# Handing x over already turned, and starting the matmul operands at differing byte offsets, in a conditional FFN kernel

## The chip, the cores and the metric

The kernel runs on one core of one Trainium2 chip. The metric is device time in microseconds (us), the median of several runs; lower is better. The engines are PE (matmul, with PEld its weight loads), DVE (vector), ACT (scalar and activation), POOL (GpSimd) and SP, which in this kernel only issues DMAs. The code is written engine by engine: each engine has its own program, and the programs meet only through semaphores, so the order inside an engine is the order written.

## The reference, cut to what matters

```
B, T, D = 4, 1024, 1024;  8 groups of LATENT = 128 columns;  FFN = 512
h    = gelu(einsum('btel,elf->btef', x as 8 groups, W1) + b1)
y    = einsum('btef,efl->btel', h, W2) + b2                  # back to D = 1024
eo   = silu(cond) @ emb_W + emb_b;   scale, shift = halves of eo
hn   = layernorm(y, ln_g, ln_b) * (1 + scale) + shift
out  = x + silu(hn) @ out_W + out_b
```

Everything is float32. To keep precision the kernel splits each matmul operand into a rounded high part (float32r) and a low rest, and does three matmuls in place of one: high by high, low weights by high, high weights by low.

## The kernel before

**Two parts.** The first part (FFN) makes y, turned so that the 128 columns of a group lie on the partitions and the tokens run along the row. It goes over 4 blocks of 1,024 tokens, one for each batch entry; in each block over 8 groups g; in each group over 4 chunks c of the 512 hidden columns. k = 4g + c counts the 32 steps of a block. Each step has on PE a `first` (W1, 6 matmuls of 512 columns into a PSUM ring slot) and a `second` (W2, 6 matmuls of 512 columns into the y PSUM), with `first` two steps ahead of `second`. The blocks are FIRST, two rounds of MIDDLE in a hardware loop, and LAST. Between the two matmul sets ACT does the gelu (L510) and DVE splits its result into g_hi (L664) and g_lo (L666); at the end of a group ACT adds b2 and writes y_stage (L543), and SP stores it to DRAM (L364).

The second part (projection) goes over 8 windows of 512 tokens with 4 row tiles each. A tile is 48 matmuls of 512 columns (L964; L977 for the last tile). There the weights loaded into the array are slices of s_hi and s_lo (128 tokens), and the moving operands are oW_hi and oW_lo. Mean and variance of the next window are two pairs of matmuls with ones_r as weights (L852, L853).

**How x gets turned.** x lies in DRAM with a token to a row. `load_x` (L303) brings a group of a block as 8 pieces of 128 tokens by 128 columns into `xin`. At k = 0 of each group PE turns the next group: `turn_x` (L820), 8 matmuls against an identity into a ring slot of its own. ACT copies that slot to `xT_raw` (L502), then rounds it to `xT_hi` (L506); DVE makes `xT_lo` (L659). There are 31 such turns: 8 start in FIRST, 16 in MIDDLE, 7 in LAST. The very first group is turned in two halves ahead of everything (L869, copied at L519, rounded at L521, rest at L650), and its matmuls are at L883. The small vectors (b1, b2, emb_b, ln_g, ln_b, cond) come in as 104 rows by six DMAs, are turned once on PE (L873) and copied to `cols` (L654).

**Other work with an order of its own.** In FIRST, SP loads the raw weights of a group two groups ahead, ACT rounds them (L533) and POOL makes the low part (L425). POOL does this in one loop: for group m it first waits for y_stage of group m - 2 and adds it to a running sum (L443), and only then splits the weights of group m. PE waits for that split before the first matmul of group m (at k = 2 of the group before). In LAST, POOL, ACT and DVE also normalise window 0 while PE still works on the FFN: SP loads y of window 0 back in two halves (L356), issued at k = 4 and k = 8 behind the load of x, and POOL centres it (L469), adds up squares (L474) and scales it (L481).

**The SP queue at the start of a group.** At k % 4 == 0 SP waits for a count of `xT_psum`, which PE raises when a turn is complete, then issues the next load of x. In LAST the load of y (L356) stands behind that wait.

**Where operands lie.** SBUF tensors are placed one after the other in the order of the `sb` calls, each at a multiple of 32 bytes. From the sizes in the code, the start of each tensor taken modulo 512 bytes is: oW_hi, oW_lo and ident 128; ones_r 32; sum_hi, sum_lo 64; and W, xT_hi, xT_lo, g_hi, g_lo, xin, and in the second part s_hi and s_lo of both windows, all 448. Every slice that a matmul takes begins a multiple of 512 bytes after the start of its tensor.

Of the kernel before, what the change touches and what calls it, by code (L numbers as in the profile page):

```python
# [5 lines left out]
P = 128  # L25
F32 = mybir.dt.float32
# [8 lines left out]
def cond_ffn_program(nc, x, cond, W1, b1, W2, b2, emb_W, emb_b, ln_g, ln_b, out_W, out_b, out):  # L35
# [3 lines left out]
    KE = cond.shape[1] // P  # L39
    NE = emb_W.shape[1] // P  # L40
    TA = T
    SUB = TA // P
# [18 lines left out]
    assert ROWS <= P  # L61

    with ExitStack() as ctx:
# [9 lines left out]
        oW_hi = sb("oW_hi", [P, G, D], F32R)  # L73
        oW_lo = sb("oW_lo", [P, G, D], F32R)
# [12 lines left out]
        vec_rows = emb_rows[:, 0:P]  # L87
# [6 lines left out]
        with ExitStack() as a:  # L94

            W = sb("W", [P, G, 4, FF], F32R, a)
            xT_hi = sb("xT_hi", [P, 2, TA], F32R, a)
            xT_lo = sb("xT_lo", [P, 2, TA], F32R, a)
            g_raw = sb("g_raw", [P, 2, TA], F32, a)
            g_hi = sb("g_hi", [P, 2, TA], F32R, a)  # L100
            g_lo = sb("g_lo", [P, 2, TA], F32R, a)
            xT_raw = sb("xT_raw", [P, TA], F32, a)
            xin = sb("xin", [P, 2, SUB, P], F32, a)
            y_stage = sb("y_stage", [P, 2, TA], F32, a)
            wraw = sb("wraw", [P, 2, 2 * FF], F32, a)
            assert D == 2 * FF == KE * P


        with ExitStack() as b:
            yb0 = sb("yb0", [P, G, TB], F32, b)  # L110
            s_lo0 = sb("s_lo0", [P, G, TB], F32R, b)
            s_hi0 = sb("s_hi0", [P, G, TB], F32R, b)
            sq = sb("sq", [P, G, TB], F32, b)
            yb1 = sb("yb1", [P, G, TB], F32, b)
            s_hi1 = sb("s_hi1", [P, G, TB], F32R, b)
            s_lo1 = sb("s_lo1", [P, G, TB], F32R, b)
            res = sb("res", [P, 2, D], F32, b)
            out_b_all = sb("out_b_all", [P, D], F32, b)
# [14 lines left out]
        vec_landed_pool = sem("vec_landed_pool")  # L133
        vec_turned = sem("vec_turned")
        cols_ready = sem("cols_ready")
# [21 lines left out]
        x0T_psum = sem("x0T_psum")  # L157
        x0_raw = sem("x0_raw")
        x0_hi = sem("x0_hi")
        x0_lo = sem("x0_lo")  # L160
        xT_psum = sem("xT_psum")
        xraw_done = sem("xraw_done")
# [102 lines left out]
        x_cols = x.rearrange("b (s p) (g l) -> b g p s l", p=P, l=L)  # L265
# [13 lines left out]
        def landed(m):  # L279
# [7 lines left out]
        small_vectors = ((R_B1, b1.rearrange("g (c p) -> (g c) p", p=P)), (R_B2, b2),  # L287
                         (R_C, cond.rearrange("b (k p) -> (b k) p", p=P)),
                         (R_EB, emb_b.rearrange("(n p) -> n p", p=P)),
                         (R_G, ln_g.rearrange("(n p) -> n p", p=P)),  # L290
                         (R_B, ln_b.rearrange("(n p) -> n p", p=P)))

# [3 lines left out]
        def _(sp):  # L296
# [5 lines left out]
            def load_x(i, g):  # L302
                sp.dma_start(xin[:, g % 2], x_cols[i, g]).then_inc(x_landed[g % 2], 16)  # L303

            for h in range(2):
                part = slice(h * SB, (h + 1) * SB)
                sp.dma_start(xin[:, 0, part], x_cols[0, 0, :, part]).then_inc(x0_landed[h], 16)
            for r0, v in small_vectors[:3]:
                sp.dma_start(vec_rows[r0:r0 + v.shape[0], :], v).then_inc(vec_landed, 16)
# [104 lines left out]
        def _(pool):  # L414
# [5 lines left out]
            for r0, v in small_vectors[3:]:  # L420
                pool.dma_start(vec_rows[r0:r0 + v.shape[0], :], v).then_inc(vec_landed_pool, 16)
# [70 lines left out]
        def _(act):  # L492
# [20 lines left out]
            for h in range(2):  # L513
                part = slice(h * BANK, (h + 1) * BANK)
                if h == 0:
                    act.wait_ge(x0T_psum, 1)
                else:
                    act.wait_ge(xT_psum, 1)
                nc.scalar.copy(xT_raw[:, part], ring(0)[:, part]).then_inc(xraw_done if h else x0_raw, 1)  # L519
                act.wait_ge(xraw_done if h else x0_raw, 1)  # L520
                nc.scalar.copy(xT_hi[:, 0, part], xT_raw[:, part]).then_inc(xhi_done if h else x0_hi, 1)  # L521
            act.wait_ge(cols_ready, 1)
# [25 lines left out]
            def body(i, kind):  # L548
                start, last = kind == FIRST, kind == LAST
                slot, _ = PLAN[kind]  # L550
                for k in range(K):
                    g = k // C
                    if ("T", g + 1) in slot and k % C == 0:
# [76 lines left out]
        def _(dve):  # L630
# [16 lines left out]
            for h in range(2):  # L647
                part = slice(h * BANK, (h + 1) * BANK)
                dve.wait_ge(xhi_done if h else x0_hi, 1)
                nc.vector.tensor_tensor(xT_lo[:, 0, part], xT_raw[:, part], xT_hi[:, 0, part].bitcast(F32),  # L650
                                        ALU.subtract).then_inc(xlo_done if h else x0_lo, 1)
                if h == 0:
                    dve.wait_ge(vec_turned, 1)
                    nc.vector.tensor_copy(cols[:], psum[:, 4, 0:ROWS]).then_inc(cols_ready, 1)  # L654
            split_w0(1)

            def rest_xT(n, g):
                dve.wait_ge(xhi_done, n + 1)
                nc.vector.tensor_tensor(xT_lo[:, g % 2], xT_raw[:], xT_hi[:, g % 2].bitcast(F32),  # L659
# [30 lines left out]
            def body(i, kind):  # L690
                last = kind == LAST
                slot, _ = PLAN[kind]
                for k in range(K):
# [15 lines left out]
                    if ("T", g + 1) in slot and k % C == 0:  # L709
                        rest_xT(G * i + g + 1, (g + 1) % G)  # L710
# [106 lines left out]
        def _(pe):  # L817
            def turn_x(slot, g):
                for s in range(SUB):
                    mm = nc.tensor.transpose(ring(slot)[:, s * P:(s + 1) * P], xin[:, g % 2, s], ident[:])  # L820
                mm.then_inc(xT_psum, 1)

# [42 lines left out]
            pe.wait_ge(ident_ready, 1)  # L865
            for h in range(2):
                pe.wait_ge(x0_landed[h], 16)
                for s in range(h * SB, (h + 1) * SB):
                    mm = nc.tensor.transpose(ring(0)[:, s * P:(s + 1) * P], xin[:, 0, s], ident[:])  # L869
                mm.then_inc(xT_psum if h else x0T_psum, 1)  # L870
            pe.wait_ge(vec_landed, 16 * 3)
            pe.wait_ge(vec_landed_pool, 16 * 3)
            nc.tensor.transpose(psum[:, 4, 0:ROWS], vec_rows[0:ROWS, :], ident[0:ROWS, 0:ROWS]  # L873
                                ).then_inc(vec_turned, 1)
# [13 lines left out]
            def body(i, kind):  # L888
# [3 lines left out]
                def take(use):  # L892
# [4 lines left out]
                    elif kind == "T":  # L897
                        pe.wait_ge(xraw_done, G * i + n + 1)
# [8 lines left out]
                for k in range(K):  # L907
                    g = k // C
                    if k % C == 0 and ("T", g + 1) in slot:

                        if g + 1 < G:

                            pe.wait_ge(x_landed[(g + 1) % 2], 16 * ((G // 2) * i + g // 2 + 1))
                        else:
                            pe.wait_ge(x_landed[0], 16 * ((G // 2) * i + G // 2))
                        turn_x(take(("T", g + 1)), (g + 1) % G)
# [6 lines left out]
                    if last and k == K_TURN:  # L923
                        ps = ring(take(("F", 0)))
                        pe.wait_ge(emb_copied, KE + 1)
# [91 lines left out]
_INS = ["x", "cond_2048", "L0_cond_W1", "L0_cond_b1", "L0_cond_W2", "L0_cond_b2", "L0_cond_emb_W",  # L1017
        "L0_cond_emb_b", "L0_cond_ln_g", "L0_cond_ln_b", "L0_cond_out_W", "L0_cond_out_b"]


# [16 lines left out]
```

## Time and profile before

| | |
|---|---|
| device time, median of 3 runs | 799.18 us (798.22 to 799.32) |
| span of the profiled execution, first to last instruction | 788.0 us |
| what lies around the span, median less span | 11.2 us |
| PE busy | 764.1 us, 97% |
| DVE, ACT, POOL busy | 624.4, 365.5, 207.8 us |

The page gives no device time of the profiled execution itself, so the 11.2 us around its span are taken from the median. A row of a timeline begins with its start and its length in us, counted from the span's start. Matmuls overlap in the records (one of 512 columns is shown some 390 ns long), so the pace of a run of matmuls is read from start to start, or from the chain of work, which counts each piece once.

### The profile page before, as it was taken

The page shows a single profiled execution, that of the slowest core. Times are in us where ns is not written, and L with a number is a line of the kernel's source. Part 1 is how long each engine was busy: PE and PEld are TensorE (multiplying, and loading weights), DVE is VectorE, ACT ScalarE, POOL GpSimd, SP SyncE. Part 2 cuts the span into 40 slices and gives each one's busy share as a digit, 9 for nine tenths or more (in the row PEclk, how much of TensorE's full clock was granted, in tenths as well). Part 3 has the DMA queues.
Part 4 walks back from the last instruction along what each step waited for, and adds up shares of the span by engine and source line. Part 5 has one row for each costly group of instructions (what it writes and reads, how often), then busy time and mean ns, then how long its engine had stood idle before and what let it go on. Part 6 is the DMA issues. An engine that isn't in the chain of part 4 may idle for free.

```text
span 788.0 us, 9365 instructions
## 1 busy us (share of the span) xinstructions
PE 764.1 (97%) x3429; PEld 610.6 (77%) x3429; DVE 624.4 (79%) x492; ACT 365.5 (46%) x360; POOL 207.8 (26%) x110
## 2 busy tenths in 40 slices
PE   7999999999999999989988999999999999999998
PEld 5878788787787877866766887888888888888886
DVE  6888879778797786899898798888788788878511
ACT  6767567576675756566742323223041322314100
POOL 3344333022040220185162132122221221222111
PEclk9999999999999999999999999999999999999999
DMA  6353344445345453341227325252523425132221
GB/s 162 94 148 116 97 138 127 164 145 175 121 130 175 135 184 106 107 160 54 82 81 266 106 86 208 81 192 76 213 107 132 161 80 210 56 108 107 106 89 72
DMA packets 60720, 101.68 MB, mean 129 GB/s; under 512 B 2856, under 2 KB 39824, under 8 KB 58512
## 3 DMA queue, kind: packets, MB, share of 16 engines
q1 hardware_dynamic: 59920, 100.71, 37.4%
q10 hardware_dynamic: 672, 0.52, 0.2%
q8 instruction: 20, 0.33, 0.2%
q14 instruction: 12, 0.10, 0.0%
q0 software_dynamic: 96, 0.02, 0.0%
HBM read 67.69 MB, written 33.55 MB: 128 GB/s over the span
## 4 chain that ended last, share of the span: by engine, by line
PE 71%; issue 11%; DVE 9%; POOL 4%; ACT 2%; DMA 2%; SPq 0%; DVEq 0%; POOLq 0%; ACTq 0%
PE psum L964 39%; PE psum L831 13%; PE psum L845 13%; DVE g_hi L664 3%; POOL W L425 2%; PE psum L820 2%; PE psum L977 1%; DVE g_lo L666 1%; POOL stat L443 1%; PE psum L860 1%; DMA yb<-y_scratch 1%; DMA xin<-in_x 1%; DVE xT_lo L659 1%; DVE yb L765 1%; DVE sq L743 1%
## 5 line engine op out<-in xcount | busy, mean ns | idle before, releaser
L510 ACT ACTIVATE g_raw<-psum,cols 128x1024 f32<-128x1024 f32 x128 | 142.8, 1117 | 121.7 <-PE psum L831 91.4
L666 DVE TENSOR_TENSOR g_lo<-g_raw,g_hi 128x1024 fp32r<-128x1024 f32 x128 | 177.8, 1389 | 4.4
L488 POOL TENSOR_TENSOR res<-res,out_b_all 128x1024 f32<-128x1024 f32 x32 | 84.2, 2633 | 281.9 <-DMA res<-in_x 281.9
L964 PE MATMUL psum<-oW_hi,s_hi 128*128 128x512 f32 x496 | 156.2, 396 | 0.0
L964 PE MATMUL psum<-oW_lo,s_hi 128*128 128x512 f32 x496 | 156.1, 395 | 0.0
L964 PE MATMUL psum<-oW_hi,s_lo 128*128 128x512 f32 x496 | 156.0, 395 | 0.0
L831 PE MATMUL psum<-xT_hi,W 128*128 128x512 f32 x508 | 141.1, 400 | 4.9 <-POOL W L425 2.5
L845 PE MATMUL psum<-g_hi,W 128*128 128x512 f32 x512 | 137.2, 390 | 0.2 <-DVE g_hi L664 0.2
L664 DVE CAST g_hi<-g_raw 128x1024 fp32r<-128x1024 f32 x128 | 112.1, 876 | 30.7 <-PE psum L845 26.5
L831 PEld LDWEIGHTS psum<-xT_hi,W 128*128 128x128 f32 x508 | 92.1, 189 | 31.9 <-issue 6.9
L845 PEld LDWEIGHTS psum<-g_hi,W 128*128 128x128 f32 x512 | 96.0, 188 | 20.9 <-DVE g_hi L664 0.7
L964 PEld LDWEIGHTS psum<-oW_hi,s_hi 128*128 128x128 f32 x496 | 93.3, 188 | 22.9
L964 PEld LDWEIGHTS psum<-oW_lo,s_hi 128*128 128x128 f32 x496 | 93.2, 188 | 22.9
L964 PEld LDWEIGHTS psum<-oW_hi,s_lo 128*128 128x128 f32 x496 | 93.2, 188 | 22.9
L614 ACT ACTIVATE sq<-yb 128x2048 f32<-128x2048 f32 x14 | 26.9, 1920 | 132.7 <-DVE yb L760 132.7
L845 PE MATMUL psum<-g_lo,W 128*128 128x512 f32 x256 | 80.2, 394 | 5.7 <-DVE g_lo L666 5.7
L831 PE MATMUL psum<-xT_lo,W 128*128 128x512 f32 x254 | 78.3, 390 | 0.0
L755 DVE TENSOR_TENSOR res<-psum,res 128x1024 f32<-128x1024 f32 x31 | 37.9, 1221 | 46.7 <-PE psum L964 46.7
L659 DVE TENSOR_TENSOR xT_lo<-xT_raw,xT_hi 128x1024 fp32r<-128x1024 f32 x31 | 44.6, 1438 | 30.7 <-ACT xT_hi L506 30.7
L599 ACT ACTIVATE yb<-yb,mod_c,mod_a 128x512 f32<-128x512 f32 x64 | 47.0, 805 | 42.2 <-DVE yb L765 42.1
L425 POOL TENSOR_TENSOR oW_lo<-wraw,oW_hi 128x512 f32 x16 | 29.8, 1884 | 133.4 <-ACT oW_hi L588 133.4
L845 PEld LDWEIGHTS psum<-g_lo,W 128*128 128x128 f32 x256 | 47.2, 188 | 19.4 <-DVE g_lo L666 10.2
(97 smaller groups left out, 689.7 us busy)
## 6 DMA issues: line engine op xcount, KB each, us to landing
y_scratch<-y_stage SPq DMA_DIRECT2D x32, 512.0 KB, 3.3
res<-in_x SPq DMA_DIRECT2D x32, 512.0 KB, 3.3
xin<-in_x SPq DMA_DIRECT2D x31, 512.0 KB, 4.9
out<-res SPq DMA_DIRECT2D x31, 512.0 KB, 2.6
yb<-y_scratch SPq DMA_DIRECT2D x7, 2048.0 KB, 8.1
wraw<-in_L_cond_emb_W SPq DMA_DIRECT2D x8, 1024.0 KB, 5.0
wraw<-in_L_cond_out_W SPq DMA_DIRECT2D x8, 512.0 KB, 4.9
wraw<-in_L_cond_W SPq DMA_DIRECT2D x14, 256.0 KB, 3.7
```

The lines of the kernel that those rows point to most:

```text
L425: nc.gpsimd.tensor_tensor(lo, raw, hi.bitcast(F32), ALU.subtract).then_inc(pw_split, 1)
L488: nc.gpsimd.tensor_tensor(res[:, t % 2], res[:, t % 2], out_b_all[:], ALU.add).then_inc(res_biased, 1)
L510: nc.scalar.activation(g_raw[:, k % 2], ring(slot), ACT.Gelu, bias=cols[:, R_B1 + k:R_B1 + k + 1]).then_inc(gelu_done, 1)
L599: return nc.scalar.activation(yb[s][:, g], yb[s][:, g], ACT.Silu, scale=mod_a[:, b, g:g + 1], bias=mod_c[:, b, g:g + 1])
L614: nc.scalar.activation(sq[:, half], yb[s][:, half], ACT.Square).then_inc(squared, 1)
L659: nc.vector.tensor_tensor(xT_lo[:, g % 2], xT_raw[:], xT_hi[:, g % 2].bitcast(F32), ALU.subtract).then_inc(xlo_done, 1)
L664: nc.vector.tensor_copy(g_hi[:, s], g_raw[:, s]).then_inc(ghi_done, 1)
L666: nc.vector.tensor_tensor(g_lo[:, s], g_raw[:, s], g_hi[:, s].bitcast(F32), ALU.subtract).then_inc(glo_done, 1)
L755: nc.vector.tensor_tensor(res[:, t % 2], proj[t % 2], res[:, t % 2], ALU.add).then_inc(out_ready, 1)
L831: mm = nc.tensor.matmul(ring(slot)[:, h * BANK:(h + 1) * BANK], W[:, g, w, cut], v[:, g % 2, h * BANK:(h + 1) * BANK], start=(n == 0), sto ...
L845: mm = nc.tensor.matmul(y_psum(g % 2)[:, h * BANK:(h + 1) * BANK], W[:, g, w, cut], v[:, k % 2, h * BANK:(h + 1) * BANK], start=(c == 0 an ...
L964: mm = nc.tensor.matmul(proj[t % 2][:, h * BANK:(h + 1) * BANK], v[:, g, cut], w[:, g, h * BANK:(h + 1) * BANK], start=(g == 0 and n == 0) ...
```

## The change

x is handed to the kernel a second time, turned (`xT`, batch by group by column by token), and the small vectors as one array of 128 partitions by 104 (`vectors`); both are made before the launch. PE turns nothing of x or of the vectors any more. `xT_raw` becomes a double buffer which the DMA fills, in place of `xin`; ACT rounds from it as soon as the load has landed. SP's wait at the start of a group is for `xlo_done` (DVE has made xT_lo) in place of `xT_psum`. The ring in PSUM has no slot for turns. Besides, unused pieces (`gap0` to `gap7`) are put between tensors, and g_raw is moved behind g_lo.

```diff
@@ def cond_ffn_program
         oW_hi = sb("oW_hi", [P, G, D], F32R)
+        sb("gap0", [P, 16])
         oW_lo = sb("oW_lo", [P, G, D], F32R)
...
             W = sb("W", [P, G, 4, FF], F32R, a)
+            sb("gap1", [P, 16], F32, a)
             xT_hi = sb("xT_hi", [P, 2, TA], F32R, a)
+            sb("gap2", [P, 16], F32, a)
             xT_lo = sb("xT_lo", [P, 2, TA], F32R, a)
+            sb("gap3", [P, 32], F32, a)
+            g_hi = sb("g_hi", [P, 2, TA], F32R, a)
+            sb("gap4", [P, 72], F32, a)
+            g_lo = sb("g_lo", [P, 2, TA], F32R, a)
             g_raw = sb("g_raw", [P, 2, TA], F32, a)
-            g_hi = sb("g_hi", [P, 2, TA], F32R, a)
-            g_lo = sb("g_lo", [P, 2, TA], F32R, a)
-            xT_raw = sb("xT_raw", [P, TA], F32, a)
-            xin = sb("xin", [P, 2, SUB, P], F32, a)
+            xT_raw = sb("xT_raw", [P, 2, TA], F32, a)
...
             s_lo0 = sb("s_lo0", [P, G, TB], F32R, b)
+            sb("gap5", [P, 32], F32, b)
             s_hi0 = sb("s_hi0", [P, G, TB], F32R, b)
             sq = sb("sq", [P, G, TB], F32, b)
             yb1 = sb("yb1", [P, G, TB], F32, b)
+            sb("gap6", [P, 64], F32, b)
             s_hi1 = sb("s_hi1", [P, G, TB], F32R, b)
+            sb("gap7", [P, 96], F32, b)
             s_lo1 = sb("s_lo1", [P, G, TB], F32R, b)
@@ ring_plan
-                if k % C == 0 and not (last and k // C + 1 == G):
-                    uses.append(("T", k // C + 1))
@@ sync
             def load_x(i, g):
-                sp.dma_start(xin[:, g % 2], x_cols[i, g]).then_inc(x_landed[g % 2], 16)
+                sp.dma_start(xT_raw[:, g % 2], xT[i, g]).then_inc(x_landed[g % 2], 16)
...
-            for r0, v in small_vectors[:3]:
-                sp.dma_start(vec_rows[r0:r0 + v.shape[0], :], v).then_inc(vec_landed, 16)
+            sp.dma_start(cols[:], vectors).then_inc(vec_landed, 16)
...
-                        wait(xT_psum, G * i + g + 1)
+                        wait(xlo_done, G * i + g + 1)
@@ gpsimd
-            for r0, v in small_vectors[3:]:
-                pool.dma_start(vec_rows[r0:r0 + v.shape[0], :], v).then_inc(vec_landed_pool, 16)
@@ scalar
-            def copy_xT(n, slot):
-                act.wait_ge(xT_psum, n + 1)
-                nc.scalar.copy(xT_raw[:], ring(slot)).then_inc(xraw_done, 1)
-
-            def round_xT(n, g):
-                act.wait_ge(xraw_done, n + 1)
-                nc.scalar.copy(xT_hi[:, g % 2], xT_raw[:]).then_inc(xhi_done, 1)
+            def round_xT(i, g):
+                s = g % 2
+                act.wait_ge(x_landed[s], 16 * ((G // 2) * i + (g + s) // 2))
+                nc.scalar.copy(xT_hi[:, s], xT_raw[:, s]).then_inc(xhi_done, 1)
...
-                        act.wait_ge(xlo_done, G * i + g + 1)
-                        copy_xT(G * i + g + 1, slot["T", g + 1])
-                        round_xT(G * i + g + 1, (g + 1) % G)
+                        round_xT(i, g + 1)
@@ tensor
-            def turn_x(slot, g):
-                for s in range(SUB):
-                    mm = nc.tensor.transpose(ring(slot)[:, s * P:(s + 1) * P], xin[:, g % 2, s], ident[:])
-                mm.then_inc(xT_psum, 1)
...
-                        turn_x(take(("T", g + 1)), (g + 1) % G)
```

By the same count as above, after the change the starts modulo 512 are: oW_hi 128, oW_lo 192; W 0, xT_hi 64, xT_lo 128, g_hi 256, g_lo 32; s_lo0 0, s_hi0 128, s_hi1 384, s_lo1 256.

## Rows read from the trace of the kernel before

**Rows 1.** The page: engines, granted clock in slices, and the chain's shares.

```profile
PE 764.1 (97%) x3429; PEld 610.6 (77%) x3429; DVE 624.4 (79%) x492; ACT 365.5 (46%) x360; POOL 207.8 (26%) x110
...
PEclk9999999999999999999999999999999999999999
...
PE 71%; issue 11%; DVE 9%; POOL 4%; ACT 2%; DMA 2%; SPq 0%; DVEq 0%; POOLq 0%; ACTq 0%
```

**Rows 2.** The chain in order of time (start, us, what): MIDDLE, then the projection.

```profile
212.40 1.36 PE psum L845 x6
...
719.03 54.60 PE psum L964 x234
```

**Rows 3.** Timeline of PE in one group of MIDDLE, turn to turn.

```profile
209.53 0.62 PE L845 MATMUL psum<-g_lo,W 128*128 128x512 f32 x2
209.99 1.03 PE L820 MATMUL psum<-ident,xin 128*128 128x128 f32 x8
210.78 1.17 PE L831 MATMUL psum<-xT_hi,W 128*128 128x512 f32 x4
...
221.76 1.03 PE L820 MATMUL psum<-ident,xin 128*128 128x128 f32 x8
```

**Rows 4.** The chain in order of time, one round of FIRST.

```profile
80.91 7.08 issue
...
88.02 1.91 POOL stat L443
...
91.14 2.29 POOL W L425
```

**Rows 5.** Waits of PE for POOL (us, times, longest).

```profile
PE psum L831 <- POOL W L425: 2.5, 5, 0.7
```

**Rows 6.** Timeline of all engines, the opening.

```profile
4.81 1.09 PE L869 MATMUL psum<-ident,xin 128*128 128x128 f32 x4 [4.81 <-DMA xin<-in_x]
5.94 0.59 ACT L519 COPY xT_raw<-psum 128x512 f32<-128x512 f32 x1 [2.94 <-PE psum L869]
6.55 0.62 ACT L521 CAST xT_hi<-xT_raw 128x512 fp32r<-128x512 f32 x1
...
6.64 1.12 PE L869 MATMUL psum<-ident,xin 128*128 128x128 f32 x4 [0.74 <-DMA xin<-in_x]
...
7.88 1.19 PE L883 MATMUL psum<-xT_hi,W 128*128 128x512 f32 x2
...
9.21 1.28 ACT L526 ACT_TABLE_LOAD   x1
9.29 1.05 PE L883 MATMUL psum<-xT_hi,W 128*128 128x512 f32 x2
...
10.14 0.63 PE L883 MATMUL psum<-xT_lo,W 128*128 128x512 f32 x1
...
10.81 1.12 ACT L510 ACTIVATE g_raw<-psum,cols 128x1024 f32<-128x1024 f32 x1 [0.32 <-PE psum L883]
...
12.19 1.03 PE L820 MATMUL psum<-ident,xin 128*128 128x128 f32 x8
...
15.06 1.09 PE L845 MATMUL psum<-g_hi,W 128*128 128x512 f32 x4
```

**Rows 7.** Loads of x by tile, issue to landing.

```profile
DMA to landing us min/median/max: 3.9/4.9/6.7
```

**Rows 8.** Timeline of LAST around the load of y.

```profile
322.04 1.12 ACT L543 ACTIVATE y_stage<-psum,cols 128x1024 f32<-128x1024 f32 x1 [0.19 <-PE psum L845]
...
324.38 1.05 ACT L506 CAST xT_hi<-xT_raw 128x1024 fp32r<-128x1024 f32 x1
324.40 0.85 SPq L356 DMA_DIRECT2D yb<-y_scratch  x1
...
325.46 1.23 DVE L659 TENSOR_TENSOR xT_lo<-xT_raw,xT_hi 128x1024 fp32r<-128x1024 f32 x1 [1.46 <-ACT xT_hi L506]
```

**Rows 9.** Timeline of DVE in LAST, with POOL at work, and between.

```profile
353.09 2.19 DVE L666 TENSOR_TENSOR g_lo<-g_raw,g_hi 128x1024 fp32r<-128x1024 f32 x1
...
356.34 0.68 DVE L664 CAST g_hi<-g_raw 128x1024 fp32r<-128x1024 f32 x1
357.05 1.23 DVE L666 TENSOR_TENSOR g_lo<-g_raw,g_hi 128x1024 fp32r<-128x1024 f32 x1
358.19 1.78 DVE L664 CAST g_hi<-g_raw 128x1024 fp32r<-128x1024 f32 x1
```

**Rows 10.** Groups of instructions by line, ACT's copies (busy us, mean ns, idle before).

```profile
L502 ACT COPY xT_raw<-psum 128x1024 f32<-128x1024 f32 x31 | 31.5, 1017 | 6.1 <-ACT y_stage L543 6.1
```

More of the change, by code:

```diff
@@ L32, with cond_ffn_program @@
 LN_EPS = 1e-5
-def cond_ffn_program(nc, x, cond, W1, b1, W2, b2, emb_W, emb_b, ln_g, ln_b, out_W, out_b, out):
+def cond_ffn_program(nc, x, xT, vectors, W1, W2, emb_W, out_W, out_b, out):
     B, T, D = x.shape
@@ L38, in cond_ffn_program @@
     C = FF // P
-    KE = cond.shape[1] // P
+    KE = emb_W.shape[0] // P
     NE = emb_W.shape[1] // P
     TA = T
-    SUB = TA // P
     NA = B * T // TA
@@ L60, in cond_ffn_program @@
     ROWS = R_C + B * KE
-    assert ROWS <= P
+    assert vectors.shape[1] == ROWS
     with ExitStack() as ctx:
@@ L302, in load_x @@
             def load_x(i, g):
[L303 removed]
+                sp.dma_start(xT_raw[:, g % 2], xT[i, g]).then_inc(x_landed[g % 2], 16)
             for h in range(2):
[L306 to L309 removed]
+                part = slice(h * BANK, (h + 1) * BANK)
+                sp.dma_start(xT_raw[:, 0, part], xT[0, 0, :, part]).then_inc(x0_landed[h], 16)
+            sp.dma_start(cols[:], vectors).then_inc(vec_landed, 16)
             load_x(0, 1)
@@ L514, in _ @@
                 part = slice(h * BANK, (h + 1) * BANK)
[L515 to L522, printed above, removed]
+                act.wait_ge(x0_landed[h], 16)
+                nc.scalar.copy(xT_hi[:, 0, part], xT_raw[:, 0, part]).then_inc(xhi_done if h else x0_hi, 1)
+            act.wait_ge(vec_landed, 16)
             act.wait_ge(cond_zeroed, 1)
@@ L552, in body @@
                     g = k // C
-                    if ("T", g + 1) in slot and k % C == 0:
-                        act.wait_ge(xlo_done, G * i + g + 1)
-                        copy_xT(G * i + g + 1, slot["T", g + 1])
-                        round_xT(G * i + g + 1, (g + 1) % G)
+                    if k % C == 0 and not (last and g + 1 == G):
+                        round_xT(i, g + 1)
                     if last and k == K_MEAN:
@@ L649, in _ @@
                 dve.wait_ge(xhi_done if h else x0_hi, 1)
-                nc.vector.tensor_tensor(xT_lo[:, 0, part], xT_raw[:, part], xT_hi[:, 0, part].bitcast(F32),
+                nc.vector.tensor_tensor(xT_lo[:, 0, part], xT_raw[:, 0, part], xT_hi[:, 0, part].bitcast(F32),
                                         ALU.subtract).then_inc(xlo_done if h else x0_lo, 1)
-                if h == 0:
-                    dve.wait_ge(vec_turned, 1)
-                    nc.vector.tensor_copy(cols[:], psum[:, 4, 0:ROWS]).then_inc(cols_ready, 1)
             split_w0(1)
@@ L658, in rest_xT @@
                 dve.wait_ge(xhi_done, n + 1)
-                nc.vector.tensor_tensor(xT_lo[:, g % 2], xT_raw[:], xT_hi[:, g % 2].bitcast(F32),
+                nc.vector.tensor_tensor(xT_lo[:, g % 2], xT_raw[:, g % 2], xT_hi[:, g % 2].bitcast(F32),
                                         ALU.subtract).then_inc(xlo_done, 1)
@@ L708, in body @@
                                               ).then_inc(emb_copied, 1)
-                    if ("T", g + 1) in slot and k % C == 0:
+                    if k % C == 0 and not (last and g + 1 == G):
                         rest_xT(G * i + g + 1, (g + 1) % G)
@@ L863, in embed @@
                 mm.then_inc(emb_chunk, 1)
[L865 to L874, printed above, removed]
             pe.wait_ge(w_split0, 1)
@@ L908, in body @@
                     g = k // C
[L909 to L915, printed above, removed]
-                        turn_x(take(("T", g + 1)), (g + 1) % G)
                     if kind == MIDDLE and k in K_EMB:
@@ L924, in body @@
                         ps = ring(take(("F", 0)))
+                        pe.wait_ge(ident_ready, 1)
                         pe.wait_ge(emb_copied, KE + 1)
@@ L1025 @@
     from concourse.bass_utils import run_bass_kernel_spmd as _run
+    x = _np.asarray(inputs["x"])
+    B, T, D = x.shape
+    vectors = [_np.asarray(inputs[n]).reshape(-1, 128) for n in
+               ("L0_cond_b1", "L0_cond_b2", "L0_cond_emb_b", "L0_cond_ln_g", "L0_cond_ln_b", "cond_2048")]
+    ins = {
+        "x": x,
+        "xT": x.reshape(B, T, D // 128, 128).transpose(0, 2, 3, 1),
+        "vectors": _np.concatenate(vectors).T,
+        "W1": inputs["L0_cond_W1"],
+        "W2": inputs["L0_cond_W2"],
+        "emb_W": inputs["L0_cond_emb_W"],
+        "out_W": inputs["L0_cond_out_W"],
+        "out_b": inputs["L0_cond_out_b"],
+    }
     nc = _bacc.Bacc("TRN2", target_bir_lowering=False, num_devices=1)
     arrays, args = {}, []
-    for name in _INS:
-        a = _np.ascontiguousarray(inputs[name])
+    for name, v in ins.items():
+        a = _np.ascontiguousarray(v)
         arrays[f"in_{name}"] = a
         args.append(nc.dram_tensor(f"in_{name}", a.shape, _mybir.dt.from_np(a.dtype), kind="ExternalInput").ap())
-    args.append(nc.dram_tensor("out", arrays["in_x"].shape, F32, kind="ExternalOutput").ap())
+    args.append(nc.dram_tensor("out", (B, T, D), F32, kind="ExternalOutput").ap())
     cond_ffn_program(nc, *args)
```

18 lines of the change are left out of this document (removed).

## The prediction

> **What bounds the kernel now.** I read the page first: PE is busy 97% of the span at the full granted clock, DVE comes next at 79%, and the chain that ends last is PE for 71% [rows 1]. Then the chain in order of time, to see where PE is not the bound, and the pace of PE where it is. In MIDDLE six matmuls of 512 columns take 1.36 us, 226.7 ns each; in the projection 234 take 54.60 us, 233.3 ns each [rows 2]. Same shape, same type, same clock, steady in both. [...]
>
> Three stretches have another bound. In FIRST a loop through POOL does: PE is let go, runs out the group, POOL adds (1.91 us) and splits the weights (2.29 us for the second half), and PE waits for it [rows 4, 5]; five rounds show the wait. In LAST, while POOL is busy, DVE pays 2.19 us in place of 1.23 for g_lo and 1.78 us for g_hi [rows 9], together 3.97 us a step, while PE needs 2 x 1.36 = 2.72: DVE bounds PE. And the opening is a chain DMA, PE, ACT, PE.
>
> **The turns.** One group in MIDDLE is 221.76 - 209.99 = 11.77 us from turn to turn [rows 3]. Its 48 matmuls at 226.7 ns are 10.88 us, so a turn costs 0.89 us. (Check: the turn begins at 209.99 and the next `first` at 210.78, 0.79 us; its four matmuls then take longer than four steady ones, which makes the rest.) What each of the 31 turns is worth depends on its place.
>
> - Turn 1 (12.19) is in the opening, counted below.
> - Turns 2 to 7 lie in FIRST in the stretch of POOL's loop. The turn is not in that loop: it stands behind the last `second` of a group, while the loop goes from there by y_stage to POOL and back to PE at k = 2. So PE waits 0.89 us longer and these six bring nothing.
> - Turn 8 (begins FIRST's last group), the 16 of MIDDLE and the first of LAST are PE-bound: 18 x 0.89 = 16.0 us.
> - The other six, in LAST, run into the stretch that DVE and POOL bound. Besides, the load of y (L356) is issued at 324.40 now, and would be issued after xT_lo: y_stage ends at 323.16, xT_hi takes 1.05, xT_lo 1.23, then two DMAs are issued, about 326.2 [rows 8]. POOL's work on window 0 begins 1.8 us later, while PE is up to two turns (1.8 us) ahead. I take 0 here, with bounds of a gain and a loss of 1.8 us.
>
> **The opening.** Now: first half landed at 4.8, turned to 5.9, copied 0.59, rounded 0.62, first real matmul 7.88 [rows 6]. After: landed about 4.8, rounded by 5.5, PE starts `first(0)` about 5.5; the second half landed by 6.6, is rounded by 7.3, and `first(0)` ends near 8.6 at the slow clock that this stretch has now (9.29 to 10.14 for two, 0.43 us each). The table load for gelu no longer waits for the turned vectors and would end near 8.9, so gelu(0) starts at 8.9, not 10.81. PE then does `first(1)` to 11.2, and, with no turn and no wait, `first(2)` to 12.6: `second(0)` at 12.6 where it is at 15.06. Gain 2.4 us. [...] The gain reaches POOL's loop with `y_stage` of group 0 and goes through it unchanged.
>
> **ACT, DVE and the queues.** ACT loses 31 copies of 1.0 us [rows 10]; it was waiting most of its time, so this costs and brings nothing by itself, and it covers the 0.89 us by which PE reaches gelu sooner. DVE does the same work in groups 10.88 us long; its work in a plain group is 4 x (0.68 + 1.23) + 1.2 = 8.8 us [rows 8, 9], and under POOL in MIDDLE two steps of a group are at 3.97: that adds some 4 us to single groups. The steps there have slack (PE waited for nothing in MIDDLE); I take 0, bound 2 us of loss. The load of x is issued later: after xT_lo instead of after the turn, about 1.8 us. From then to the next rounding there are about 8.3 us (10.88 less the 2.6 from y_stage's end to the issue), and the slowest landing is 6.7 [rows 7]. Hidden, with 1.6 us to spare. Rows of x become 4 KB instead of 512 bytes in DRAM, so landing should not get slower.
>
> At an unchanged pace: 799.2 - 2.4 - 16.0 = 780.8 us.
>
> **The byte offsets.** The trace has the two paces, at two distances. [...] Distance = start of the moving operand less start of the weights, modulo 512: it is 0 in the whole FFN (448 and 448), pace 226.7; it is 192 in the whole projection (128 and 448), pace 233.3 [rows 2]. Nothing else that I find differs. [...] After the change the distances are 64, 128, 256 and 32 in the FFN; in the projection 0, 64, 128 and 192 in windows with s_hi0, and 256, 320, 384, 448 in the others. [...] Between the ends I take 224.5 ns for both parts: the row of distance 0, a little less because the distance now changes every matmul or two and no collision repeats. About 1,060 FFN matmuls are PE-bound (18 whole groups, half of six, the opening): 1,060 x 2.2 ns = 2.3 us. Of the projection some 60 lie beside a wait for DVE: 1,476 x 8.8 ns = 13.0 us. Together 15.3 us.
>
> [...]
>
> [...]
>
> **The rivals.**
> [...]
> 2. The offsets do nothing; the two paces come from something else in the two parts. 781 us.
> 3. The offsets hurt: distance 0 was the good one, and the mixed distances bring the FFN to 233.3 and leave the projection. 1,060 x 6.6 ns = 7 us: 788 us. For: the only row at distance 0 is the faster one.
> 4. Slower than before: the load of x comes too late. ACT stands in `round_xT` for the landing, and behind it on ACT are the gelu of the group, then DVE's splits, then `second`. Each us over 8.3 us of landing costs 24 groups a us; to use up the 34 us of gain it must take 8.3 + 34 / 24 = 9.7 us, against 6.7 at worst today [rows 7]. At 10.2 us it gives about 811 us.
>
> **How the numbers follow.** Forecast (pace 222 to 227 in both parts) 0.42, own range 758 to 773; rival 1, 0.22; rival 2, 0.19; rival 3, 0.13; rival 4, 0.04. The predicted time is 799.2 - 2.4 - 16.0 - 15.3 = 765.5 us. The range goes down to rival 1 less the bounds of the opening and LAST, 742, and up to rival 2 with 2 us for LAST or MIDDLE, 783; outside are rivals 3 and 4 and the edge of 1. 0.2% (1.6 us) is about what a measurement here can tell from no change. All cases but rival 4 are faster: faster 0.95, same 0.01, slower 0.04.
>
> **What the profile after would show.** No L820 rows and groups of MIDDLE about 10.8 us long; if they are 11.7, the turns' time went elsewhere. In FIRST PE's waits for POOL grow to about six of 1.3 us. `second(0)` starts near 12.6. The load of y in LAST is issued after xT_lo, and PE's waits for DVE there grow. [...] The window with s_hi0 and the one with s_hi1 should differ in pace if the distance matters. A wait of ACT for the DMA of x, which no row has now, would be rival 4. The prediction is wrong most easily in the pace, which is 15 of its 34 us and rests on two rows.

## The result, and the profile after

The changed kernel takes 785.86 us, median of 4 runs (784.70 to 786.49), beside 798.83 us (798.22 to 799.32) of the kernel before, timed beside it: a ratio of 0.9847 with an interval from 0.9821 to 0.9872. It is faster by 13 us, 1.5%, where 34 us were forecast, and the time lies above the range of 742 to 783.

The page of the kernel after, its counterpart to [rows 1] (busy time, granted clock, chain):

```profile
span 783.5 us, 8764 instructions
PE 745.5 (95%) x3172; PEld 587.0 (75%) x3172; DVE 639.7 (82%) x491; ACT 332.9 (42%) x327; POOL 211.0 (27%) x107
PEclk9999999999999999999899989999999999999999
PE 64%; DVE 15%; issue 13%; POOL 4%; ACT 2%; DMA 1%; SPq 0%; DVEq 0%; ACTq 0%; POOLq 0%
```

PE lost 18.6 us of work, yet its share of the chain fell from 71% to 64%: it now waits more. Two slices show a granted clock below full. The profiled execution took 785.26 us, so 1.8 us lie around its span, not the 11.2 of the forecast.

The same landmarks in both profiled executions, in us from the span's start (each is the start of an instruction of PE, read from the timeline):

| | before | after | length before | length after |
|---|---|---|---|---|
| `second(0)` | 15.06 | 12.08 | 15.06 | 12.08 |
| MIDDLE begins (group 8) | 113.14 | 112.39 | 98.08 | 100.31 |
| LAST begins (group 24) | 311.33 | 300.33 | 198.19 | 187.94 |
| first tile of the projection | 413.48 | 401.40 | 102.15 | 101.07 |
| last tile | 773.46 | 769.10 | 359.98 | 367.70 |

So the opening gave 3.0 us, FIRST lost 2.2, MIDDLE gave 10.3, LAST 1.1, and the projection lost 7.7. Together that is the 4.5 us between the two profiled spans, not the 13 us between the medians: the profiled execution of the kernel before was a shorter one than those that were timed (below). In the opening, the timeline after (beside [rows 6]): x is rounded at 4.44 as it lands, `first(0)` starts at 5.83 (it waits for W, not for x), and `second(0)` at 12.08.

```profile
4.44 0.62 ACT L480 CAST xT_hi<-xT_raw 128x512 fp32r<-128x512 f32 x1 [1.48 <-DMA xT_raw<-in_xT]
5.83 1.22 PE L821 MATMUL psum<-xT_hi,W 128*128 128x512 f32 x2 [5.83 <-DVE W L599]
12.08 1.09 PE L793 MATMUL psum<-g_hi,W 128*128 128x512 f32 x4
```

The pace is in the chain in order of time, the view of [rows 2]. In a plain group of MIDDLE (240 us) six matmuls take 1.37 to 1.40 us, where they took 1.36:

```profile
252.31 1.37 PE psum L779 x6
253.69 1.39 PE psum L793 x6
255.07 1.39 PE psum L779 x6
256.46 1.40 PE psum L793 x6
```

and at the end of the projection 234 matmuls take 54.20 us, 231.6 ns each, where they took 233.3:

```profile
700.23 0.23 PE psum L800
700.46 0.23 PE psum L801
700.70 13.89 PE psum L893 x60
715.06 54.20 PE psum L893 x234
769.26 11.12 PE psum L906 x48
```

48 matmuls of a plain group of MIDDLE take 11.09 us, 231.0 ns each. The two parts have met in the middle: the FFN is 4.3 ns a matmul dearer, the projection 1.7 ns cheaper. The four windows with s_hi0 and the four with s_hi1 do not differ (231.5 to 231.7 ns in the steady pieces of each), though the prediction wanted them to if the distance matters. From the starts and the three products that the code does, their distances are 0, 64 and 128 with s_hi0 and 256, 320 and 384 with s_hi1, each 256 more. (The prediction also lists 192 and 448; they belong to low by low, which no matmul does.)

Waits, the view of [rows 5]:

```profile
PE psum L800 <- DVE sum_lo L702: 11.0, 6, 3.9
PE psum L779 <- POOL W L392: 9.3, 6, 1.7
PE psum L793 <- DVE g_lo L619: 5.8, 9, 0.9
```

Two grew. The six waits for POOL in FIRST were forecast as "about six of 1.3"; they are 1.02 to 1.67. The first row is the new one: the matmuls that sum s for the next window's mean (L800) wait 11.0 us in the projection for DVE. In the profile before, the same wait had only two entries, of 3.37 and 0.95 us; two later profiles, one of the kernel before and one of it with all small DMAs on SP, have four each (7.1 and 7.9 us).

### The profile page after: what moved, and what is told of

Read it like the earlier page. It is cut to its first block, busy times and chain, and to the rows that moved or that the text cites. A ratio compares the mean times of both kernels' runs of the same rounds, so it can differ in the third digit from the quotient of the medians.

```text
span 783.5 us, 8764 instructions
## 1 busy us (share of the span) xinstructions
PE 745.5 (95%) x3172; PEld 587.0 (75%) x3172; DVE 639.7 (82%) x491; ACT 332.9 (42%) x327; POOL 211.0 (27%) x107
## 4 chain that ended last, share of the span: by engine, by line
PE 64%; DVE 15%; issue 13%; POOL 4%; ACT 2%; DMA 1%; SPq 0%; DVEq 0%; ACTq 0%; POOLq 0%
PE psum L893 34%; PE psum L779 13%; PE psum L793 13%; DVE g_hi L617 3%; DVE sq L694 2%; DVE sum_lo L702 2%; POOL W L392 2%; DVE sq L696 1%; PE psum L906 1%; DVE g_lo L619 1%; POOL stat L410 1%; PE psum L808 1%; DVE xT_lo L612 1%; DVE sum_hi L700 1%; DMA yb<-y_scratch 1%
## 5 line engine op out<-in xcount | busy, mean ns | idle before, releaser
L619 DVE TENSOR_TENSOR g_lo<-g_raw,g_hi 128x1024 fp32r<-128x1024 f32 x128 | 183.1, 1431 | 4.4
L455 POOL TENSOR_TENSOR res<-res,out_b_all 128x1024 f32<-128x1024 f32 x32 | 85.6, 2677 | 288.0 <-DMA res<-in_x 288.0
L779 PE MATMUL psum<-xT_hi,W 128*128 128x512 f32 x508 | 141.0, 400 | 10.2 <-POOL W L392 9.3
L617 DVE CAST g_hi<-g_raw 128x1024 fp32r<-128x1024 f32 x128 | 111.4, 871 | 38.8 <-PE psum L793 34.7
L793 PE MATMUL psum<-g_hi,W 128*128 128x512 f32 x512 | 141.1, 398 | 1.3 <-DVE g_hi L617 1.3
L779 PEld LDWEIGHTS psum<-xT_hi,W 128*128 128x128 f32 x508 | 95.1, 190 | 41.5 <-issue 18.4
L793 PE MATMUL psum<-g_lo,W 128*128 128x512 f32 x256 | 81.8, 400 | 5.9 <-DVE g_lo L619 5.8
L779 PE MATMUL psum<-xT_lo,W 128*128 128x512 f32 x254 | 79.9, 395 | 0.6 <-DVE xT_lo L612 0.6
L779 PEld LDWEIGHTS psum<-xT_lo,W 128*128 128x128 f32 x254 | 48.0, 189 | 12.0 <-DVE xT_lo L612 1.3
```

The source lines that it names most:

```text
L455: nc.gpsimd.tensor_tensor(res[:, t % 2], res[:, t % 2], out_b_all[:], ALU.add).then_inc(res_biased, 1)
L617: nc.vector.tensor_copy(g_hi[:, s], g_raw[:, s]).then_inc(ghi_done, 1)
L619: nc.vector.tensor_tensor(g_lo[:, s], g_raw[:, s], g_hi[:, s].bitcast(F32), ALU.subtract).then_inc(glo_done, 1)
L779: mm = nc.tensor.matmul(ring(slot)[:, h * BANK:(h + 1) * BANK], W[:, g, w, cut], v[:, g % 2, h * BANK:(h + 1) * BANK], start=(n == 0), sto ...
L793: mm = nc.tensor.matmul(y_psum(g % 2)[:, h * BANK:(h + 1) * BANK], W[:, g, w, cut], v[:, k % 2, h * BANK:(h + 1) * BANK], start=(c == 0 an ...
```

## The experiments

Each group of kernels ran on one chip beside the kernel before, whose median drifted from one group to the next (795.59, 791.59 and 792.14 us), so ratios are compared. There are three questions: what the offsets do, what lies around the span, and what the waits in the projection and in FIRST cost.

**Without the gaps.** `gap0` to `gap7` go, everything else of the change stays.

```diff
-        sb("gap0", [P, 16])
...
-            sb("gap7", [P, 96], F32, b)
```

> The changed kernel without gap0 to gap7: all FFN operands again at distance 0, all of the projection at 192; no turns. Theory A (the distance between moving operand and weights sets the pace): FFN back to 226.7 ns, projection to 233.3 ns, plain groups of MIDDLE 10.88 us in place of 11.09. POOL's loop in FIRST back to 12.5 us a round. Span 783.5 less 32 x 0.2 and less 6 x 0.5 us, some 775 to 779 us; less if DVE's new waits in the projection (4 of 1.3 us, 1 of 3.9 us) go as well. Rival (the pace change comes from the missing turns or the moved x buffer, not from the gaps): the pace stays 231 ns in both parts and the time within 0.3% of the changed kernel's.

Measured: 775.98 us (775.04 to 781.16), ratio 0.9762 (0.9731 to 0.9792). A plain group of MIDDLE takes 10.88 us and a matmul of the projection 233.3 ns: both paces of the kernel before are back.

```profile
710.44 54.60 PE psum L885 x234
```

The turned input alone brings 2.4%, 19.6 us against the kernel before beside it, where 18.4 were forecast at an unchanged pace. The gaps take some of it away. The rounds of FIRST, though, stay at 12.92 us where 12.5 was expected: it is not the gaps that made them longer.

**Distance 0 everywhere.** On top of that, two pads of 192 bytes move the operands so that the moving operands and the weights start at one place modulo 512 in the projection too.

```diff
+            sb("pad_a", [P, 48], F32, a)
             W = sb("W", [P, G, 4, FF], F32R, a)
...
+            sb("pad_b", [P, 48], F32, b)
             yb0 = sb("yb0", [P, G, TB], F32, b)
```

> As e1_no_gaps, but with 192 bytes of padding ahead of W and ahead of yb0, so that the projection's operands too are at distance 0 (all start at 128 modulo 512). Theory A: projection at 226.7 ns as the FFN: 6.6 ns x 1,476 = some 10 us faster than e1. Rival (the two paces of before come from something else in the two parts): projection stays at 233.3 ns, same time as e1.

Measured: 772.04 us (771.30 to 776.68), ratio 0.9712 (0.9682 to 0.9743). The chain of this kernel:

```profile
707.83 53.04 PE psum L887 x234
760.87 10.89 PE psum L900 x48
```

53.04 / 234 = 226.7 ns in the projection, from 233.3, with nothing changed but where the tensors lie. That would be worth 9.7 us over 1,476 matmuls. The whole kernel gained 4.5 us by its profile, 0.5% by its ratio: the waits for sum_lo rose from 7.7 us (5 times) to 13.0 us (7 times), because PE reaches the sum sooner while DVE does not. Another bound eats part of the gain of the pace.

**What lies around the span.** A rival for the missing gain (theory O) was that the 11.2 us around the span come from the small DMAs that POOL issues, and go with them. Two kernels test it: the kernel before with these three issued by SP, and the kernel after with three such DMAs issued by POOL into `emb_rows`, which is set to zero later:

```diff
-            for r0, v in small_vectors[3:]:
-                pool.dma_start(vec_rows[r0:r0 + v.shape[0], :], v).then_inc(vec_landed_pool, 16)
...
```

> The kernel before, with the three small DMAs of POOL (emb_b, ln_g, ln_b) issued by SP behind its own three; nothing else changed. Median less span is 11.2 us in the kernel before and 1.8 us in the changed one (one execution each). Theory O (a DMA issued by POOL costs time around the span): the device time less the span falls to some 2 us, span the same within 1 us, time some 9 us less. Rival (the profiled execution of before is not of the length of the others, or the number of DRAM tensors makes it): difference and time stay as in the kernel before.

```diff
+            for n in range(3):
+                pool.dma_start(emb_rows[:, n * ROWS:(n + 1) * ROWS], vectors).then_inc(pool_dma_landed, 16)
```

> The changed kernel with three DMAs issued by POOL at the place where the kernel before has them (they bring the vectors into emb_rows, which nothing uses before it is set to zero, so the work is the reference's). Theory O: time 9 us more than the changed kernel, about 795 us, with the span the same within 1 us. Rival: time within 0.3% of the changed kernel.

Measured: 794.93 us (790.24 to 797.64), ratio 0.9988 (0.9960 to 1.0016), and 782.23 us (776.98 to 784.64), ratio 0.9851 (0.9819 to 0.9884). Neither moved the time, and 1.8 us lie around the span of both (797.21 less 795.4, 777.08 less 775.3). Theory O fell. Both spread over 7 us, and the profiled run of the second, one of its shortest, waits for sum_lo three times, 5.7 us in all, where the kernel after has 11.0 in six; its projection takes 359.17 us from the first tile to the last, where after takes 367.70. That made the waits the suspect for the spread.

**The kernel before, once more.**

> The kernel before, unchanged, for a second profile. Theory R (POOL's bias adds and DVE's sums for the mean meet on their shared access in the projection, and which comes first differs from execution to execution; the execution profiled first was one where PE hardly waited): span 792 to 797 us, equal to 788.0 until the projection, with tiles of the projection 1 to 4 us longer where 788.0 had none, and PE waiting for DVE's sum_lo there. Rival (the 11 us between span and median are time around the span): span 788 again and the time 799.

Measured: 791.26 us (789.04 to 793.42). The profiled execution took 793.42, its span 791.6: 1.8 us around it again. Its waits have a row that the first profile has at 4.3 us:

```profile
PE psum L852 <- DVE sum_lo L749: 7.1, 4, 3.4
```

With the same 1.8 us around it, the execution behind the prediction's profile took about 789.8 us (788.0 + 1.8), less than those that were timed with it. So 9.4 of the 11.2 us were no overhead but the difference between two executions.

**How the race goes.** DVE and POOL meet in the first tile of a window (in window 0, in the second). DVE folds the eight groups of the next window into one and splits the sum (L694 to L702), so that PE can take the mean; POOL adds the bias to `res` (L455). In the kernel after, window 2, DVE and below it POOL:

```profile
505.36 2.28 DVE L694 TENSOR_TENSOR sq<-yb 128x2048 f32<-128x2048 f32 x1
507.68 3.31 DVE L696 TENSOR_TENSOR sq<-sq 128x1024 f32<-128x1024 f32 x1
511.02 0.69 DVE L698 TENSOR_TENSOR stat<-sq 128x512 f32<-128x512 f32 x1
511.75 2.54 DVE L700 CAST sum_hi<-stat 128x512 fp32r<-128x512 f32 x1
514.32 0.69 DVE L702 TENSOR_TENSOR sum_lo<-stat,sum_hi 128x512 fp32r<-128x512 f32 x1
505.41 4.49 POOL L455 TENSOR_TENSOR res<-res,out_b_all 128x1024 f32<-128x1024 f32 x1 [13.36 <-DMA res<-in_x]
511.60 2.41 POOL L455 TENSOR_TENSOR res<-res,out_b_all 128x1024 f32<-128x1024 f32 x1 [1.70 <-DMA res<-in_x]
```

L696 takes 3.31 us and L700 2.54, while POOL's instruction runs, and POOL's own first one takes 4.49. To see what they take alone, POOL is made to wait, on the base of distance 0, until the two parts of the sum are there:

```diff
+            def add_bias(i, summed):
+                if summed:
+                    pool.wait_ge(sum_split, 4 * i + 2)
...
+            with pool.Fori(0, NB - 1) as i:
+                add_bias(i, True)
+            add_bias(NB - 1, False)
```

> e2_distance_zero, and POOL adds the bias to the tiles of a window only after DVE has made the sums of that window for the mean. Theory R: DVE's sums are no longer drawn out (7 to 9.7 us back to some 5.5), PE's waits for sum_lo in the projection go (four or five of 1.3 to 2.3 us and one of 3 to 4), 772 to some 763 us, and the runs lie closer together. Rival (DVE is late for another reason, or POOL's adds then come too late for the tile's end): no gain, or slower.

Measured: 757.70 us (757.07 to 758.06), ratio 0.9567 (0.9545 to 0.9589), and the row of waits for sum_lo is gone. The same place in its timeline:

```profile
488.43 2.28 DVE L694 TENSOR_TENSOR sq<-yb 128x2048 f32<-128x2048 f32 x1
490.75 1.23 DVE L696 TENSOR_TENSOR sq<-sq 128x1024 f32<-128x1024 f32 x1
492.01 0.69 DVE L698 TENSOR_TENSOR stat<-sq 128x512 f32<-128x512 f32 x1
492.73 0.43 DVE L700 CAST sum_hi<-stat 128x512 fp32r<-128x512 f32 x1
493.19 0.69 DVE L702 TENSOR_TENSOR sum_lo<-stat,sum_hi 128x512 fp32r<-128x512 f32 x1
494.07 4.76 POOL L451 TENSOR_TENSOR res<-res,out_b_all 128x1024 f32<-128x1024 f32 x2 [18.52 <-DVE sum_lo L702]
```

L696 is at 1.23, L700 at 0.43, and POOL's two instructions at 2.38 each. PE no longer waits, so the delay of `res` does not reach it. In the kernel of distance 0 without this wait the same place went the other way round: POOL began 0.02 us ahead of DVE and took 2.40 us, and DVE's first instruction took 4.53 in place of 2.28. The gain over distance 0 alone is 1.45% by the ratios, 11.5 us, for 13.0 us of waits in that profile. The timed runs lie within 1.0 us, where they lay within 5.4. That the race makes the spread is not shown by it: one run makes most of the 5.4 (the other four lie within 0.8), and the next two kernels, one with the race and one without, spread over 2.7 and 2.6. L702, too, takes 0.69 us alone (above) and 2.71 beside L455 (below). What the two engines share, of which theory R speaks, is shown by no trace; the traces show that the instruction of one of them, or of both, takes longer while they run side by side.

**The weights split first.** In FIRST, on the base of distance 0, POOL splits the weights of group m before it waits for y_stage of m - 2.

```diff
 for m in range(1, G + 2):
+    if m < G:
+        pool.wait_ge(wraw_landed[m % 2], landed(m))
...
     if m >= 2:
         g = m - 2
         pool.wait_ge(y_staged, g + 1)
...
-    if m >= G:
-        continue
-    pool.wait_ge(wraw_landed[m % 2], landed(m))
...
```

> e2_distance_zero, and in FIRST POOL splits the weights of group m before it waits for y_stage of group m - 2. Theory P (POOL's loop hides the turns of FIRST): rounds of FIRST fall from 12.9 to 10.9 us, six of them, 12 us less: 772 to some 760 us. Rival (DVE or the load of the weights bounds FIRST as well): rounds stay above 12 us.

Measured: 763.23 us (762.97 to 765.70), ratio 0.9638 (0.9617 to 0.9660). No wait of PE for POOL is left in FIRST, and MIDDLE begins at 105.49 us, from 112.08. The saving is 6.6 us, where six rounds from 13.0 to 10.9 would give 12.6: only three rounds are 10.9, the others 11.3 to 12.5, and the first grew from 11.9 to 13.9, with DVE in the chain (L617 and L619 of the kernel after). DVE is the next bound there.

**Both together.**

> e6 and e7 together: if both theories hold and add up, some 751 us, faster than the kernel before and the changed one.

Measured: 750.94 us (750.41 to 752.99), ratio 0.9489 (0.9462 to 0.9515). The two savings, 0.0145 and 0.0074, add up (0.0223 measured, 0.0219 as a sum), since they lie in different stages. This kernel is faster than both kernels of the case, and with PE's waits for sum_lo and for POOL gone it is a good base for the offsets.

**The gaps on the clean base.** The changed kernel's own eight gaps, in place of the two pads.

> The changed kernel with its own gaps, and POOL's two orders of e8_both. It differs from e8_both in the byte offsets alone. Theory A (offsets set the pace; mixed distances bring about 231 ns in both parts): 4.3 ns x some 2,700 PE-bound matmuls = 11 to 12 us more than e8_both, some 762 us, with no waits for sum_lo in the projection. Rival (the gaps cost mainly by what they shift between DVE and POOL): within 3 us of e8_both.

Measured: 762.29 us (761.76 to 763.85), ratio 0.9620 (0.9596 to 0.9643).

**One distance for all matmuls.** Distance means, as in the prediction, the start of the moving operand less the start of the weights, modulo 512. A gap between W and xT_hi sets it for the FFN, `pad_b` for the projection. At 64 (128 and 256 have other sizes; `gap_g`, 512 bytes, shifts no distance, and 256 goes without it):

```diff
             W = sb("W", [P, G, 4, FF], F32R, a)
+            sb("gap", [P, 16], F32, a)
             xT_hi = sb("xT_hi", [P, 2, TA], F32R, a)
...
+            sb("gap_g", [P, 128], F32, a)
             g_hi = sb("g_hi", [P, 2, TA], F32R, a)
...
-            sb("pad_b", [P, 48], F32, b)
+            sb("pad_b", [P, 160], F32, b)
```

> e8_both with every moving operand 64 bytes past its weights modulo 512, in both parts (constant distance 64). Theory M (a constant distance settles at a low pace and only the mixing of distances costs): 226.7 ns as at 0. Theory D (each distance has its own price): another pace than 226.7 and 233.3 possible, the same in both parts; at 233.3 ns the time would be some 17 us over e8_both.

> As e10 with a constant distance of 128. Theory M: 226.7 ns, time of e8_both. Theory D: its own pace, the same in both parts.

> As e10 with a constant distance of 256. Theory M: 226.7 ns, time of e8_both. Theory D: its own pace, the same in both parts.

Measured, with the kernels that fix the other rows; "projection" is the last run of 234 matmuls in the chain, divided by 234:

| distance | us | ratio to before | plain group of MIDDLE | projection, ns a matmul |
|---|---|---|---|---|
| 0 (both together) | 750.94 | 0.9489 (0.9462 to 0.9515) | 10.88 us | 226.7 |
| 64 | 758.05 | 0.9570 (0.9544 to 0.9596) | 10.99 us | 229.0 |
| 128 | 764.23 | 0.9644 (0.9619 to 0.9669) | 11.16 us | 232.4 |
| 192 (projection of before and without the gaps) | | | | 233.3 |
| 256 | 751.05 | 0.9485 (0.9459 to 0.9512) | 10.88 us | 226.7 |
| mixed, the gaps | 762.29 | 0.9620 (0.9596 to 0.9643) | 11.09 us | 231.6 |

The rows of the chain behind the last column: for 64,

```profile
688.16 53.58 PE psum L894 x234
```

for 128,

```profile
695.17 54.37 PE psum L894 x234
```

for 256,

```profile
682.24 53.04 PE psum L893 x234
```

and with the gaps,

```profile
693.62 54.20 PE psum L898 x234
```

The pace follows the distance in both parts of the kernel, with different tensors in each. Since a kernel of one constant distance has its own pace, it is not only the mixing that costs, and theory M falls. The pace is best at 0 and 256 and grows from 64 to 128 to 192. That 0 and 256 are alike fits with the two kinds of window of the kernel after, whose distances differ by 256 and whose paces do not; 320 and 384 were not tried alone. Mixed distances are not cheaper than their parts: with s_hi0 the projection has 0, 64 and 128 in equal shares, whose rows average 229.4 ns, and takes 231.6. With nothing else to hide them, the gaps cost 762.29 - 750.94 = 11.4 us against distance 0. The paces alone give, as an estimate with the prediction's counts, 1,060 x 4.3 + 1,476 x 4.9 ns = 11.8 us.

## Why the prediction was wrong

**The step that failed** is the price of the mixed distances: "Between the ends I take 224.5 ns for both parts", with the reason "because the distance now changes every matmul or two and no collision repeats". Measured: 231.0 ns in the FFN and 231.6 in the projection. The 224.5 ns and the lower of the two ends between which it was taken were the author's estimate: no run shows them, nor anything that collides. The lowest steady pace of any run was 226.7 ns. By the prediction's own counts that is +4.6 us for 1,060 matmuls of the FFN where -2.3 stood, and -2.5 us for 1,476 of the projection where -13.0 stood: +2.1 us in place of -15.3. By the ratios the gaps cost even more, 0.9847 against 0.9762, 0.85% or some 7 us, with an uncertainty of 3 to 4; the two profiles differ by 4.1 us. On one chip, the kernel after with three more DMAs of POOL took 782.23 and the one without gaps 775.98. What the gaps cost beyond the paces there stays open. The forecast of 765.5 us with 17 to 22 us put back is 783 to 788 us, around the result.

It drew the right variable from the two paces (the distance between the two operands, with 0 the cheaper) and then left the rows for an argument. **Rival 3** (the offsets hurt, distance 0 was the good one, 788 us) was the case that came. It had the mechanism right for the FFN and was given 0.13. Against rival 2 (the offsets do nothing) the 226.7, 229.0 and 232.4 ns of one kernel in which pads alone changed are conclusive. Rival 1, a pace of 216 ns, was given 0.22; that pace was the author's estimate, and no distance tried went below 226.7. The low end of the range, 742 us, is rival 1 less bounds of the opening and of LAST: no run shows such a pace, and the opening gave 3.0 us, LAST 1.1.

**The turns** were right: 18 at 0.89 us were forecast as 16.0. The 16 groups of MIDDLE take 198.19 us before and 185.16 without the gaps, 13.0 us or 0.81 a turn, where 14.2 stood. With the gaps they take 187.94.

**The opening** was right in its mechanism and gave 3.0 us in place of 2.4. x was rounded sooner than taken (4.44), but `first(0)` began at 5.83, later than taken, since it waited for W, and ended at 8.55, as taken. What gave the rest is `first(1)`: it was over at 10.68, not 11.2, because from 10.2 on its matmuls started 0.23 us apart and no longer 0.43. The prediction calls 0.43 us the slow clock; the profile has the granted clock at 1.00 there in both kernels, so where this pace comes from is open. The moment of the change varies: in the other kernels with the turned input `second(0)` begins between 11.8 and 13.0.

**FIRST** was half right. The turns there bring nothing, as said, and PE's waits grew as said. But the rounds became longer, from 12.50 to 12.99 us, and the stage lost 2.2 us where 0.9 of gain stood (turn 8). "ACT, DVE and the queues ... 0" missed this: with no copy out of PSUM, x is rounded sooner, so DVE starts xT_lo just ahead of POOL's split and the two run side by side. DVE:

```profile
89.42 1.89 DVE L612 TENSOR_TENSOR xT_lo<-xT_raw,xT_hi 128x1024 fp32r<-128x1024 f32 x1 [0.36 <-ACT xT_hi L470]
91.23 1.78 DVE L617 CAST g_hi<-g_raw 128x1024 fp32r<-128x1024 f32 x1
```

and POOL, whose split now takes 3.94 us (1.72 us for the second half, in the chain); before, the same two took 3.52 us from 89.90, ahead of DVE's xT_lo at 90.24:

```profile
88.31 1.92 POOL L410 TENSOR_TENSOR stat<-stat,y_stage 128x512 f32<-128x512 f32 x1 [7.15 <-ACT y_stage L502]
90.19 3.94 POOL L392 TENSOR_TENSOR W<-wraw,W 128x512 fp32r<-128x512 f32 x2
```

That POOL's loop is the bound is shown by the kernel that splits first; that the order of these two instructions makes the 0.49 us a round is read from the timelines and was not tried by itself. It comes with the turned input, not with the gaps: without them the rounds are 12.92 and the same split takes 3.94 us.

**LAST** was right: 0 was taken for the six turns and 0.9 for the first, and it gave 1.1 us. DVE bounds it, at 19.79 us of 20 from 380 to 400. But the load of y is not issued later, though the prediction had it so. The wait that the change puts ahead of it asks for the xT_lo of the group before, already there, and SP's queue goes on right behind y_stage (end 312.30), as it did before [rows 8]:

```profile
312.37 0.40 SPq L333 DMA_DIRECT2D y_scratch<-y_stage  x1
312.88 0.40 SPq L273 DMA_DIRECT2D xT_raw<-in_xT  x1
313.54 0.63 SPq L325 DMA_DIRECT2D yb<-y_scratch  x1
```

The load of x, which the prediction had 1.8 us later by the same reading, is not late either: its median landing is 4.5 us (4.9 before [rows 7]). Rival 4 has nothing to stand on: no row shows ACT waiting for x in MIDDLE.

**The projection** was taken as free of anything but its pace. It lost 7.7 us against the first profile, though steady tiles shortened by 0.08 us. The race of DVE and POOL, hidden in most windows of that profile, came out in six of after's. How much of it is chance from run to run shows in the other profiles: from its first tile to its last the projection takes 359.98, 363.38 and 366.71 us in three executions of the kernel before (one of them with its small DMAs on SP), and 367.70 and 359.17 in two with the change (the second with three more DMAs). That the change made the race worse is not shown.

**The base of the sum** was 799.2 us, with 11.2 us around the span. That did no harm to the differences, but the profile's own execution was a short one, and its projection had few waits.

## What to carry to other kernels

Read the pace of each long run of matmuls in ns apiece, and if two parts with one shape differ, compare where the moving operand and the weights start; make them equal, not different (226.7 ns a matmul at distance 0 here, 233.3 at 192), and trust no pace that no row shows. Where two engines slow each other, as DVE and POOL do here, the order in which they arrive decides who pays: with POOL 0.02 us ahead, DVE's first instruction took 4.53 us and POOL's 2.40; with DVE 0.05 us ahead, POOL's took 4.49 and DVE's first 2.28. And a wait that makes the less urgent one come second can be worth as much as the whole change (11.5 us against 13). A gain that is forecast from a faster engine stops at the next bound: 9.7 us of pace gave 4.5 us while the race was still there. And before a difference between two profiles is explained, take a second profile of the same kernel: here two executions of one kernel differed by 3.6 us.

## What the runs showed of the hardware that was not expected

The pace of this kernel's float32r matmuls of 512 columns, each with its own weights, depends on the distance of their operands in SBUF: 226.7 ns at 0, 229.0 at 64, 232.4 at 128, 233.3 at 192, 226.7 at 256. In the kernel after, the matmuls of `second` have g_hi at 256 and g_lo at 32 and take 1.38 to 1.40 us for six, though distance 256 throughout takes 1.36. Whether distance 32 is that dear, or a change of distance is, was not tried.

A wait of PE cost twice here: its own 3.91 us, and a granted clock of 0.51 around its end. Window 1 of the kernel after, by stretches (the columns are busy us of PE, PEld, DVE, ACT, POOL, then the granted clock, DMA share and GB/s):

```profile
455.00:460.00 5.00, 5.00 (x23) 4.07 (x22) 4.97 (x4) 0.00 (x0) 1.90 (x1) 1.00 0.56 210
460.00:464.00 4.00, 2.08 (x9) 1.33 (x8) 3.90 (x4) 0.00 (x0) 1.89 (x2) 1.00 0.84 328
464.00:471.00 7.00, 5.01 (x12) 3.99 (x13) 5.68 (x3) 1.42 (x1) 1.39 (x1) 0.51 0.45 190
471.00:476.00 5.00, 5.00 (x23) 4.03 (x22) 4.15 (x3) 3.69 (x3) 0.00 (x0) 1.00 0.26 105
```

The wait is that for sum_lo, which POOL had made late:

```profile
463.23 2.71 DVE L702 TENSOR_TENSOR sum_lo<-stat,sum_hi 128x512 fp32r<-128x512 f32 x1
463.02 2.37 POOL L455 TENSOR_TENSOR res<-res,out_b_all 128x1024 f32<-128x1024 f32 x1 [2.11 <-DMA res<-in_x]
```

PE stood for 3.91 us, until 465.99. From 464 to 471 us the granted clock was 0.51, and PE did 12 matmuls in its 5.0 busy us. The tile took 17.41 us where the same one took 12.86 in the first profile of before, whose mean clock was 0.998 (after: 0.989). It is nothing that the change brought: the kernel before with its DMAs on SP waits 3.24 us at the same place, has the clock at 0.51 from 480 to 484 us, and needs 16.78 us for the tile. Of the other five waits for sum_lo in after, the one of 3.46 us was followed by a lower clock too (0.72 from 418 to 424 us), the four of 0.6 to 1.2 us were not; without the gaps one of 1.95 us was (0.50 from 463 to 465 us). The clock is also down at 386 to 392 us in LAST (0.50), where DVE is the bound.
